# The turned maxima of the attention queries: 16 small transposes and a copy, or one transpose, a copy and a DMA

## The reference, cut to what matters

```python
xn = _layernorm(x)
qkv = xn @ Wqkv.T                     # q, k, v: 16 heads of 16, q and k rotated
scores = einsum('bhqd,bhkd->bhqk', q, k) * scale
scores = where(causal, -inf, scores)
attn = softmax(scores, axis=-1)       # exp(score - the row's maximum) / sum
out = einsum('bhqk,bhkd->bhqd', attn, v) @ Wout.T
x = x + out + experts(xn) + shared(xn)
```

## Time and profile before

| | us |
|---|---|
| median of 3 runs | 922.68 (922.35 to 1379.95) |
| the profiled execution | 912.92 |
| its span in the trace | 910.9 |
| TensorE busy in the span | 832.9 (91%) |
| VectorE busy | 621.0 (68%) |
| ScalarE, GpSimd busy | 496.9, 501.1 (55% each) |

### The profile page before, as it was taken

How to read it: one execution, slowest core, us unless ns; L and a number is a source line. 1 busy time by engine, 2 the same in 40 slices (tenths; PEclk the granted TensorE clock), 3 DMA queues, 4 the chain that set the end, 5 groups by cost and what they waited for, 6 DMA issues and landing times.

```text
span 910.9 us, 17583 instructions
## 1 busy us (share of the span) xinstructions
PE 832.9 (91%) x5282; PEld 454.6 (50%) x5282; DVE 621.0 (68%) x1247; ACT 496.9 (55%) x1214; POOL 501.1 (55%) x636
## 2 busy tenths in 40 slices
PE   2799987698989999989999999988999999999997
PEld 1466654233343433368888887863343343433444
DVE  4778887878876787755555555546788777888322
ACT  2456543154656566634445444445676767667662
POOL 5445640399998503056667666526888888800000
PEclk9999997789999999999999999998999999999999
DMA  7005544610000132047778777874585555600011
GB/s 220 0 31 178 192 155 141 187 53 18 1 19 1 26 80 71 1 127 238 221 223 248 232 228 243 131 115 75 73 174 91 71 88 72 91 7 1 13 37 45
DMA packets 81792, 96.11 MB, mean 106 GB/s; under 512 B 12835, under 2 KB 73251, under 8 KB 81699
## 3 DMA queue, kind: packets, MB, share of 16 engines
q0 software_dynamic: 19968, 31.47, 19.4%
q1 hardware_dynamic: 44838, 46.75, 17.3%
q10 hardware_dynamic: 16896, 16.78, 5.4%
HBM read 61.11 MB, written 33.82 MB: 104 GB/s over the span
## 4 chain that ended last, share of the span: by engine, by line
PE 52%; issue 16%; DVE 11%; DMA 7%; POOLq 6%; POOL 4%; ACT 2%; DVEq 1%; ACTq 0%
PE bank L1183 12%; PE bank L1166 12%; PE vector_banks L1142 10%; DMA turned<-normed_rows,tok_i 6%; DVE mpart L948 6%; POOLq L567 5%; PE vector_banks L1055 4%; PE vector_banks L1034 3%; PE bank L1055 3%; POOL turned L575 2%; PE vector_banks L1203 2%; POOL slot_w L569 2%; PE bank L1071 2%; PE bank L1169 1%; PE vector_banks L1145 1%
## 5 line engine op out<-in xcount | busy, mean ns | idle before, releaser
L948 DVE TENSOR_REDUCE mpart<-vector_banks 128x2 f32<-128x1024 f32 (+3 forms) x320 | 330.6, 1062 | 94.4 <-PE vector_banks L1142 54.3
L698 ACT ACTIVATE probs<-bank 128x512 f32<-128x512 f32 (+3 forms) x428 | 213.6, 537 | 132.0 <-PE bank L1166 63.7
L1166 PE MATMUL bank<-turned 99*128 99x512 bf16 (+3 forms) x640 | 207.8, 357 | 13.6 <-ACT probs L698 4.5
L575 POOL DMA_INDIRECT turned<-normed_rows,tok_i x128 | 125.3, 979 | 131.1 <-PE vector_banks L1034 81.5
L1142 PE MATMUL vector_banks<-turned 96*128 96x512 bf16 (+3 forms) x640 | 185.7, 360 | 11.3 <-DVE mpart L948 10.8
L590 POOL DMA_INDIRECT res<-expert_rows,slot_i x96 | 148.8, 1550 | 39.8 <-issue 28.4
L1166 PEld LDWEIGHTS bank<-turned 99*128 99x128 bf16 x640 | 59.0, 98 | 182.0 <-ACT probs L698 87.1
L698 ACT ACTIVATE at_first<-bank 128x512 f32<-128x512 f32 (+3 forms) x212 | 106.3, 531 | 71.9 <-PE bank L1169 36.8
L1261 PE MATMUL vector_banks<-xn_all,probs 128*128 x512 | 135.0, 386 | 4.5 <-issue 1.7
L1183 PE MATMUL bank<-probs,V 128*32 128x512 f32 (+3 forms) x856 | 101.9, 548 | 0.0
L1261 PEld LDWEIGHTS vector_banks<-xn_all,probs 128*128 128x128 f32 x512 | 87.2, 190 | 17.3 <-issue 9.3
(11 more groups left out here) (153 smaller groups left out, 997.1 us busy)
## 6 DMA issues: line engine op xcount, KB each, us to landing
expert_rows<-probs ACTq DMA_DIRECT2D x32, 512.0 KB, 4.4
term_rows<-at_first SPq DMA_DIRECT2D x96, 128.0 KB
turned<-term_rows SPq DMA_DIRECT2D x32, 384.0 KB, 4.7
xn_all<-wexp SPq DMA_DIRECT2D x32, 384.0 KB, 4.0
normed_rows<-xn_all SPq DMA_DIRECT2D x4, 512.0 KB, 5.5
turned<-normed_rows,tok_i POOLq DMA_INDIRECT x128, 3.8
out<-res SPq DMA_DIRECT2D x16, 128.0 KB, 1.7
res<-x SPq DMA_DIRECT2D x1, 1536.0 KB, 8.7
```

The source lines that it names most:

```text
L575: gp.indirect_dma_start(xg[:, n % XR, :], None, xn_dram, bass.IndirectOffsetOnAxis(ap=tok_i[:, n:n + 1], axis=0)).then_inc(rows_in[n % XR] ...
L698: A(PT[v // 2 % 6][:, v % 2, 0:width], bank[A_BANK[step][0]][:, 0:width], ACT.Exp).then_inc(s["scalar_bank_read"], 1)
L948: V.tensor_reduce(mpart[:, t % TPC, 2 * j:2 * j + 2, p], ring[:, :, 0:w], AX.X, ALU.max).then_inc(s["vector_bank_read"], 1)
L1166: last = mm(ring[:, 0:CH - off], k_turned(parity(g), slice(0, KM), h, kb * P, P), q_turned(slice(0, KM), h, c * CH + off, CH - off), start ...
```

## The change: what it does

`mcat` now holds its 48 columns as (term, head, tile). "mt" is one transpose of the 48 columns into partitions 0 to 47 of a ring piece; VectorE copies these 48 rows of 128 values into one of two tiles `turned_max`; and a new function `store_max(g, c)` has SP's queue wait for that copy and then put the 48 rows, 256 bytes each, into the three rows of the chunk's queries by a DMA. So that the three rows are in one piece for a chunk, the queries in `QK` now lie chunk by chunk (`q_turned`, `load_terms`). The chunk's first "st" waits for the DMA (`max_stored`) where it waited for the copy. The order moves three things: the strips of the chunks of group 0 are due two ticks earlier, "mt" comes two ticks after "mc" and no longer four, and at a chunk's start the "pv" of the block before last goes ahead of the first "st".

```diff
--- before.py
+++ after.py
@@ -102,8 +102,7 @@
     scores, score_goals = [], [(0, 0)]
     for c in range(1, NCH):
         scores += strips(0, c)
-        score_goals.append((4 * (key_blocks.index((0, c, 0)) - 1), len(scores)))
-    score_goals[-1] = (4 * (key_blocks.index((0, NCH - 1, 0)) - 1), len(scores))
+        score_goals.append((4 * key_blocks.index((0, c, 0)) - 6, len(scores)))
     for g in range(1, NG):
         for c in range(NCH):
             scores += strips(g, c)
@@ -136,7 +135,7 @@
                 order.append(step)
                 if step[0] == "mx" and step == strips(step[1], step[2])[-1]:
                     order.append(("mc", *step[1:3]))
-                    later.append((at + 4, ("mt", *step[1:3])))
+                    later.append((at + 2, ("mt", *step[1:3])))
             fill[2] = upto
         for _ in range(2):
             if chain:
@@ -161,6 +160,8 @@
             order.append(later.pop()[1])
             pending = []
             before = len(order)
+        if kb == 0 and len(pending) == 2:
+            values(pending.pop(0))
         order.append(("st", g, c, kb, 0))
         some()
         order.append(("st", g, c, kb, 1))
@@ -345,7 +346,8 @@
         QK = turned[:, :].bitcast(BF16)
 
         def q_turned(rows, j, q0, w):
-            return QK[rows, j * T + q0:j * T + q0 + w]
+            at = q0 // CH * HG * CH + j * CH + q0 % CH
+            return QK[rows, at:at + w]
 
         def k_turned(par, rows, j, k0, w):
             at = (1 + par) * HG * T + j * T + k0
@@ -365,7 +367,8 @@
         mpart = sb("mpart", [P, TPC, HG, NCH])
         mneg = sb("mneg", [P, TPC * HG])
         mrem = sb("mrem", [P, TPC * HG])
-        mcat = sb("mcat", [P, TPC * HG, 3], BF16)
+        mcat = sb("mcat", [P, KM - KQ, TPC * HG], BF16)
+        turned_max = [sb(f"turned_max{b}", [(KM - KQ) * TPC * HG, P], BF16) for b in range(2)]
         oT = sb("oT", [P, CH])
         rden = sb("rden", [P, TPC, HG])
 
@@ -386,7 +389,7 @@
             sig_exp pick_ready counted counts_read ranked ranks_read owner_ready owner_psum owner_row_ready plan_ready slots_ready
             routed weights_stored hot_made hot_used tok_ready slot_w_made
             vector_bank_full vector_bank_read scalar_bank_full scalar_bank_read
-            v4_ready mcat_ready pv_done o_read
+            v4_ready max_stored mcat_ready pv_done o_read
             exp_x_psum exp_x_ready gu_done gate_ready exp_h_ready exp_hT_psum exp_hT_ready y_done y_read weights_in written""".split()
         s = {n: sem(n) for n in names}
         rows_in = [sem(f"rows_in{b}") for b in range(XR)]
@@ -416,15 +419,27 @@
 
             def load_terms(kind, g, c):
 
-                at, arrived = (0, q_in[c]) if kind == 0 else ((1 + parity(g)) * HG * T, k_in[parity(g)][c])
-                sp.dma_start(QK[0:KQ, at:at + HG * T].rearrange("p (h q) -> p h q", q=T)[:, :, c * CH:(c + 1) * CH],
-                             term_rows[kind, g * HG:(g + 1) * HG, :, :, c * CH:(c + 1) * CH].rearrange("h s d t -> (s d) h t")
+                if kind == 0:
+                    to = QK[0:KQ, c * HG * CH:(c + 1) * HG * CH].rearrange("p (h q) -> p h q", q=CH)
+                else:
+                    to = QK[0:KQ, (1 + parity(g)) * HG * T:(2 + parity(g)) * HG * T].rearrange("p (h q) -> p h q", q=T)
+                    to = to[:, :, c * CH:(c + 1) * CH]
+                arrived = k_in[parity(g)][c] if kind else q_in[c]
+                sp.dma_start(to, term_rows[kind, g * HG:(g + 1) * HG, :, :, c * CH:(c + 1) * CH].rearrange("h s d t -> (s d) h t")
                              ).then_inc(arrived, 16)
 
             def store_weights(quarter):
                 sp.wait_ge(s["routed"], quarter + 1)
                 rows = xn_dram[quarter * QT4 * P:(quarter + 1) * QT4 * P, :].rearrange("(t p) d -> p t d", p=P)
                 sp.dma_start(rows[:, :, D:XW], wgt[:, quarter * QT4:(quarter + 1) * QT4, :]).then_inc(s["weights_stored"], 16)
+
+            def store_max(g, c):
+
+                sp.wait_ge(s["vector_bank_read"], D_AT["mt", g, c] + 1)
+                m = MC_AT["mc", g, c]
+                if m:
+                    sp.wait_ge(s["max_stored"], 16 * m)
+                sp.dma_start(QK[KQ:KM, c * HG * CH:(c + 1) * HG * CH], turned_max[m % 2][:, :]).then_inc(s["max_stored"], 16)
 
             def used(g, c):
 
@@ -436,6 +451,8 @@
                 sp.dma_start(rows[:, :, 0:D], xn_all[:, quarter * QT4:(quarter + 1) * QT4, :]).then_inc(s["xn_stored"], 16)
                 if quarter:
                     store_weights(quarter - 1)
+                if quarter == 3:
+                    store_max(0, 0)
                 sp.wait_ge(s["terms_read"], 2 * QT4 * (quarter + 1))
                 for kind in range(2):
                     for place, n in enumerate(SLOT_TERM[kind]):
@@ -471,23 +488,32 @@
             for b in range(NB):
                 load(b, b, True)
             for c in range(NCH):
+                if c + 1 < NCH:
+                    store_max(0, c + 1)
+                if c == NCH - 1:
+                    store_max(1, 0)
                 used(0, c)
                 load_terms(0, 1, c)
             for c in range(NCH):
                 load_terms(1, 2, c)
             for c in range(NCH - 1):
+                store_max(1, c + 1)
                 used(1, c)
                 load_terms(0, 2, c)
             with sp.Fori(1, E // NB) as i:
                 for b in range(NB):
                     load(NB * i + b, b)
+            store_max(2, 0)
             used(1, NCH - 1)
             load_terms(0, 2, NCH - 1)
             for c in range(NCH):
                 load_terms(1, 3, c)
             for c in range(NCH):
+                store_max(*((2, c + 1) if c + 1 < NCH else (3, 0)))
                 used(2, c)
                 load_terms(0, 3, c)
+            for c in range(1, NCH):
+                store_max(3, c)
             for t in range(NT):
                 sp.wait_ge(s["vector_bank_read"], D_AT["oM", t] + 1)
                 sp.dma_start(out[t * P:(t + 1) * P, :], res[:, t, :]).then_inc(s["written"], 16)
@@ -954,21 +980,23 @@
                     elif step[0] == "mc":
                         c = step[2]
                         dve.drain()
-                        V.tensor_reduce(mneg[:, :].rearrange("p (t h) -> p t h", h=HG), mpart[:, :, :, 0:c + 1], AX.X, ALU.max)
+                        V.tensor_reduce(mneg[:, :].rearrange("p (h t) -> p t h", h=HG), mpart[:, :, :, 0:c + 1], AX.X, ALU.max)
                         dve.drain()
-                        V.tensor_scalar(mcat[:, :, 0], mneg[:, :], -1.0, None, ALU.mult)
+                        V.tensor_scalar(mcat[:, 0, :], mneg[:, :], -1.0, None, ALU.mult)
                         dve.drain()
-                        V.scalar_tensor_tensor(out=mrem[:, :], in0=mneg[:, :], scalar=-1.0, in1=mcat[:, :, 0],
+                        V.scalar_tensor_tensor(out=mrem[:, :], in0=mneg[:, :], scalar=-1.0, in1=mcat[:, 0, :],
                                                op0=ALU.mult, op1=ALU.subtract)
                         dve.drain()
-                        V.tensor_copy(mcat[:, :, 1], mrem[:, :])
+                        V.tensor_copy(mcat[:, 1, :], mrem[:, :])
                         dve.drain()
-                        V.tensor_tensor(mcat[:, :, 2], mrem[:, :], mcat[:, :, 1], ALU.subtract).then_inc(s["mcat_ready"], 1)
+                        V.tensor_tensor(mcat[:, 2, :], mrem[:, :], mcat[:, 1, :], ALU.subtract).then_inc(s["mcat_ready"], 1)
                     elif step[0] == "mt":
                         _, g, c = step
                         dve.wait_ge(s["vector_bank_full"], n + 1)
-                        V.tensor_copy(QK[KQ:KM, 0:HG * T].rearrange("p (h q) -> p h q", q=T)[:, :, c * CH:(c + 1) * CH],
-                                      ring[KQ:KM, :, :].rearrange("p a b -> p (a b)").bitcast(BF16).rearrange("p (h q) -> p h q", q=CH)
+                        m = MC_AT["mc", g, c]
+                        if m >= 2:
+                            dve.wait_ge(s["max_stored"], 16 * (m - 1))
+                        V.tensor_copy(turned_max[m % 2][:, :], ring[0:(KM - KQ) * TPC * HG, 0, 0:P // 2].bitcast(BF16)
                                       ).then_inc(s["vector_bank_read"], 1)
                     elif step[0] == "oT":
                         t = step[1]
@@ -1147,17 +1175,13 @@
                     elif step[0] == "mt":
                         _, g, c = step
                         pe.wait_ge(s["mcat_ready"], MC_AT["mc", g, c] + 1)
-                        for j in range(HG):
-                            for t in range(TPC):
-                                k = j % 2 * TPC + t
-                                last = turn(ring[KQ:KM, j // 2, :].bitcast(BF16)[:, k * P:(k + 1) * P],
-                                            mcat[:, t * HG + j, :], identb[:, :])
-                        last.then_inc(full, 1)
```

(4 more changed lines are left out.)

## The result

The changed kernel took 952.89 us (median of 4 runs, 948.83 to 953.86), the kernel before 922.51 us (median of 4 runs that contain the three above; one of them, 1379.95 us, was disturbed and is left out of the comparison). The ratio is 1.0335 with a 95% interval of 1.0313 to 1.0357: slower by some 31 us. I had forecast 923 us and a range up to 936. The profiled execution took 953.82 us, its span 952.0.

A forecast was written before the change was run, and what follows sets the result against it. TensorE sets the pace in attention, with VectorE holding it up at places. From the profiled execution, 912.92 - 7.5 + 0.3 + 7.5 + 0.5 = 913.7 us; with the median's 9.8 offset 923.5, rounded to 923; range 909 to 936.

The forecast's parts named there:

- term of the moved "mt": At "mt", two ticks after "mc": TensorE's savings less new waits, 7.5 us gained, bounds nothing and 15.
- the DMA at (0, 1): First "st" of (0, 1): TensorE waits for the small DMA behind four expert loads, 7.5 us lost, bounds 5 and 10.5.
- What is removed: Each "mt": one transpose for 16 and a smaller copy; TensorE and VectorE each shed about 0.95 us per step.
- last chunks of a group: (0, 3), (1, 3), (2, 3), (3, 3): waits of TensorE outweigh the savings, together 1.1 us lost.
- (1, 2), (2, 2) and (3, 2): Terms ready 1.84 us ahead of "mt", so two ticks fit in; each keeps 0.95 us, together 2.9 gained.
- seven others: (0, 2) and chunks 0 and 1 of groups 1 to 3: 0.7 us gained each, 4.9 in all.
- every arrival turned into a wait: Lower bound of the gain from the moved "mt": nothing gained.
- The DMA's landing: Small DMA from issue to landing: 2.0 us, covered by five ticks and the "pv" ahead of the first "st".
- second rival: Landing above about 2.5 us delays first "st" of (0, 2), (0, 3), (2, 3), (3, 3): 12 us slower, 935; chance 0.2.
- The rivals: Full TensorE gain and cheap SP queue, 6 to 9 us faster (0.3); late small DMA, 12 slower (0.2).
- each mt only trades work for a wait: Gain near nothing, SP's wait at (0, 1) remains: 7 us slower, 930; counted within the forecast's 0.45.
- The 2% that I gave as 5%: Whole kernel slower by over 2%, over 941 us: chance 0.05.

The follow-up runs named there:

- sixth experiment: The kernel of 4 with the one transpose done sixteen times: 925.87 us, ratio 1.0084 against 0.9962.
- second profile of before: The kernel before, unchanged, profiled a second time: span 917.1 us.
- second experiment: The changed kernel with "mt" four ticks after "mc", not two: 927.06 us, ratio 1.0071.
- experiments 1: The kernel before with "mt" two ticks after "mc", not four: 939.21 us, ratio 1.0194.
- third experiment: The changed kernel with the new DMAs of (0, 1), (1, 1), (2, 1) and (3, 1) moved forward in SP's queue: 940.87 us, ratio 1.0184.
- 4: The changed kernel with both "mt" four ticks after "mc" and the new DMAs moved forward in SP's queue: 917.87 us, ratio 0.9962.
- seventh: The kernel of 4 without the "pv" ahead of a chunk's first "st": 917.28 us, ratio 0.9986.
- eighth: The kernel of 4 with group 0's strips due two more ticks earlier and "mt" six ticks after "mc" in groups 1 to 3: 910.31 us, ratio 0.9907.
- ninth experiment: The second experiment's kernel with only the DMA of (0, 1) moved ahead of the plan wait and expert loads: 921.58 us, ratio 1.0005.
- experiment 10: The changed kernel with seven unused matmuls of 512 columns ahead of each wait for the split maxima: 947.49 us, ratio 1.0287.

## Why the prediction was wrong

The step that failed is the term of the moved "mt": 7.5 us gained, where the waits alone used up the whole gain and the slower matmuls behind them made it a loss. The other large term, the DMA at (0, 1), held. I take the terms in their order.

*What is removed.* The sizes were right: 0.216 us for the transpose, 0.206 for the copy. That the 0.95 us per step counts in full or nearly so was tested by the sixth experiment: 8 to 11 of 15 us, so half to three quarters.

*What the moved "mt" takes back: this term failed, in sign.* I saw that waits would come and worked them out at three chunks, and concluded that they only eat part of the gain: 7.5 us left. The step failed twice.

First, in the number of the waits. At the last chunks of a group they came about as I had put them (1.4 us at (0, 3) where I had 1.9; 2.1 to 2.3 at the others where I had some 2.2). But at (1, 2), (2, 2) and (3, 2), to which I gave the full 0.95 because "two ticks fit in", TensorE waited 1.4 to 1.9 us, and at the seven others, to which I gave 0.7, 1.1 to 2.1. All waits of TensorE for VectorE at "mt" were 12.5 us in the second profile of before (10.0 for `mpart`, 2.5 for `mcat`) and are 31.3 in the changed kernel (6.5 and 24.8): 18.8 us more, against 15.2 us of TensorE's work and 3.0 us of waits for the copy that went away. That is the sum's lower bound, "every arrival turned into a wait", and not its middle. At the three chunks the error was the tick: I had priced two ticks at their mean of 0.73 us, and the two in question hold an output's four transposes, a "pv" of 1.06 us and a strip. In the kernel before, at (3, 2), they run from the end of the strip at 799.65 to the "mt" at 803.21, 3.6 us:

```profile
799.05 0.60 PE L1142 MATMUL vector_banks<-turned 96*128 96x512 bf16 x2
...
800.69 1.06 PE L1183 MATMUL bank<-probs,V 128*32 128x512 f32 x8
...
802.55 0.61 PE L1142 MATMUL vector_banks<-turned 96*128 96x512 bf16 x2 [0.48 <-DVE mpart L948]
803.21 1.05 PE L1034 MATMUL vector_banks<-identb,mcat 128*3 128x128 bf16 x16
```

Second, the prediction has no term for the clock, and so none for what TensorE does after a wait. This is the wait of (3, 2) in the changed kernel, granted clock in the column before the DMA share:

```profile
828.00:832.00 4.00, 3.98 (x33) 1.45 (x31) 3.64 (x4) 3.07 (x7) 0.00 (x0) 1.00 0.00 0
832.00:835.50 3.50, 1.79 (x13) 0.68 (x9) 3.11 (x8) 2.32 (x5) 0.00 (x0) 0.99 0.00 0
835.50:842.30 6.80, 6.42 (x21) 2.16 (x22) 3.13 (x6) 1.96 (x4) 0.00 (x0) 0.51 0.01 2
842.30:850.00 7.70, 7.70 (x58) 2.84 (x56) 5.28 (x6) 5.09 (x11) 0.00 (x0) 1.00 0.01 3
```

TensorE is half idle from 832.0 to 835.5 and then has 6.8 us at the lower clock, in which a "pv" of eight matmuls takes 1.94 us where the next two take 1.07 and 1.06 us:

```profile
837.74 1.94 PE L1207 MATMUL bank<-probs,V 128*32 128x512 f32 x8
...
842.72 1.07 PE L1207 MATMUL bank<-at_first,V 128*32 128x512 f32 x8
...
845.47 1.06 PE L1207 MATMUL bank<-probs,V 128*32 128x512 f32 x8
```

The 40 "st" up to the first one of (3, 2) took 33.6 us, in the second experiment 30.2: a wait of 1.9 us cost 3.4. Not every wait was paid so: of the eight "mt" in the second part of attention, waits of 1.8 to 2.3 us, six were followed within 2 us by the lower clock, those of (2, 2) and (2, 3) were not (1.00 from 713.1 to 720.0 and from 760.9 to 768.0). In the second profile of before, with waits of at most 1.1 us at the same places, the clock is 1.00 from 632 to 904 us. The trace of before had a sign of it, too: behind the waits around the "mt" of (0, 1) it shows a granted clock of 0.50 from 182 to 188 us.

Measured, the digit costs 17 us on the old form and 20 to 26 on the new (experiments 1; 3 to 4, and 2; by the ratios and by the medians). Less the 8 to 11 that the removed work is worth, some 9 to 18 us were lost where I had 7.5 gained.

*The DMA's landing.* Taken at 2.0 us, it is 2.3, read from the chain at (0, 0) below (start, us). Over the profiles with the new DMA it was 2.2 to 2.4 us wherever it could be read with little beside it. The second rival, which decides from 2.5, did not come in: the changed kernel has no wait at its four places. But its reason holds at one of them: at (2, 3), beside GpSimd's gathers, the landing took 3.1 us in the sixth experiment, 2.5 in the seventh and 3.5 in the eighth, and there the cover decides. 256-byte pieces did no harm that shows. The Trainium skill's fixed cost of about 2 us, page "DMA: Bandwidth & Descriptors", section "Anatomy of one DMA", lies 0.2 to 0.4 us below these landings, and that fit is for GpSimd's path.

```profile
148.74 2.29 DMA turned<-turned_max
```

*(0, 0)*: 0.3 us forecast; from "terms ready" to the first "st" it was 3.0 us (148.1 to 151.1), not 2.6 (146.2 to 148.8 in the second profile of before): 0.4 to 0.5 us.

*(0, 1)*: mechanism and place right, and the size near. I had 7.5 us. The stretch lost 10.6, but 3.5 came back up to (0, 3), and its "mt" also waited longer (2.0 us, not 0.6). The wait for the DMA itself was 6.1, and `plan_ready` came 6.4 us later than before, counted from the first "st" of (0, 0) (32.8 us behind it, not 26.4), where I gave it 2.5. TensorE worked at a clock of 0.65 in this stretch, 0.85 in the kernel before. Taking the DMA out of its place was worth 6 us (ninth experiment), all places together 9 to 14.

*(2, 1)*: 0.5 forecast, 2.8 measured, because the small DMA landed 10.9 us after its issue (8.6 to 10.6 in the second, ninth and tenth experiments, with waits of 1.0 to 2.1 us). What is queued ahead in the same queue decides: moved ahead of the five loads, in the third experiment, it held nothing up. At (1, 1) TensorE did not wait for it, as forecast.

*The base.* The profiled execution from which I made the sum was a short one, by 5.4 us in a stretch that the change does not touch. I carried the offset of 9.8 us over to the median, which was right.

*The rivals.* Neither was it. The one that I had counted into the forecast's edge, "each mt only trades work for a wait", came true as far as it goes (18.8 us of waits for 18.2 us of work and waits), and was still priced without the clock. The 2% that I gave as 5% was crossed by two terms at once.

## What to carry to other kernels

- A wait of 1.5 to 2 us on the engine that sets the pace can be paid twice: look at the granted clock in the few us behind such waits in the trace at hand, and price every new one with that. Moving a step earlier than its inputs can be ready is a new wait, even where the mean length of a step leaves room: price the very steps that it is moved over.
- A small DMA in a fixed queue costs what stands ahead of it: list the waits and transfers before it, and put it ahead of every one that does not need to be first.
- Separate the order from the form. Here the form was worth about half a per cent, near the noise, and the one digit in the order that came with it cost some two; with a later "mt" and the DMAs moved forward the same idea ended 0.9% faster than before, half of which the old form could have had too.

## What the runs showed of the hardware

- Matmuls added into a wait, results unused, shortened a stretch of 300.7 us by 13.3, while the time at the lower of the two clocks fell from 109 to 68 us over the kernel (experiment 10). The median of the whole gained only 4 to 5 us.
- A "pv" of eight matmuls took 1.94 us at a granted clock of 0.5 and 1.06 us at 1 (changed kernel, 837.7 and 845.5 us). The clock fell behind six of eight waits of 1.8 to 2.3 us.
- A DMA of 48 rows of 256 bytes within SBUF took 0.73 us to issue on SP's queue and 2.2 to 2.4 us from issue to landing with little beside it, 3.0 us behind one expert load of 384 KB (changed kernel, 193.4), 2.5 to 3.5 us beside GpSimd's gathers at (2, 3), and 10.9 us behind five loads of 384 KB that were issued in the 3 us before.
- Two profiles of the kernel before differed by 6.2 us in span, of which 5.4 lay in one stretch, 25.1 us at a clock of 1.00 in one and 30.5 us at 0.91 in the other. What starts it is open.
